# Writing out the turn loops of five graph layers and dropping a memset between gathers

## The reference, cut to what matters

```python
e = leaky_relu(alpha_s[src] + alpha_d[dst], 0.2)
m = segment_max(e, dst)
ex = exp(e - m[dst])
s = segment_sum(ex, dst)
alpha = ex / (s[dst] + 1e-16)
out = segment_sum(h[src] * alpha[:, :, None], dst)
```

## Time and profile before

| | us |
|---|---|
| timed, median of 3 runs | 7401.44 (7400.56 to 7405.69) |
| profiled execution, first to last instruction | 8931.6 |
| PE busy | 5412.5 (61%) |
| DVE busy | 4963.7 (56%) |
| ACT busy | 3871.5 (43%) |
| GpSimd busy | 5847.5 (65%) |
| mean granted TensorE clock | 0.745 |

### The profile page before, as it was taken

One profiled execution on the slowest core, in us unless ns is written; L12 is line 12 of the kernel. 1 busy time (PEld: TensorE's weight loads), 2 busy tenths in 40 slices (PEclk: granted clock), 3 DMA queues, 4 the chain that ended last, 5 costly groups with the idle time before them and its releaser, 6 DMA issues. The chain is left out here.

```text
span 8931.6 us, 130458 instructions
## 1 busy us (share of the span) xinstructions
PE 5412.5 (61%) x23088; PEld 4000.6 (45%) x23089; DVE 4963.7 (56%) x11653; ACT 3871.5 (43%) x9075; POOL 5847.5 (65%) x8186
## 2 busy tenths in 40 slices
PE   6442365666535656664676666658888754666665
PEld 5431244444424444443455555435555533444443
DVE  6444355555545555554677777744444445555556
ACT  2220255455424554552244444335555533454444
POOL 0555677777747777775467666657777765777774
PEclk9555677777767777776788988868888866777777
DMA  4112233333313333331466666423333323333332
GB/s 143 49 49 52 75 95 95 95 96 95 86 44 97 96 95 95 96 97 33 127 176 178 177 176 175 129 64 99 100 101 100 101 53 101 99 99 99 98 98 74
DMA packets 580940, 894.72 MB, mean 100 GB/s; under 512 B 307359, under 2 KB 357708, under 8 KB 580448
## 3 DMA queue, kind: packets, MB, share of 16 engines
q0 software_dynamic: 245984, 649.30, 26.7%
q1 hardware_dynamic: 334448, 218.84, 8.9%
q10 hardware_dynamic: 416, 25.60, 0.9%
HBM read 859.36 MB, written 59.47 MB: 103 GB/s over the span
## 5 line engine op out<-in xcount | busy, mean ns | idle before, releaser
L2002 POOL DMA_INDIRECT ad_ring<-tab_qv,ad_idx x808 | 770.7, 954 | 506.4 <-issue 217.6
L1515 POOL DMA_INDIRECT at_ring_0a<-tab_s,at_idx_0a x808 | 774.3, 958 | 430.9 <-PE at_po_0a L1680 219.2
L2396 POOL DMA_INDIRECT ae_ring<-tab_a,ae_idx x808 | 777.9, 963 | 423.0 <-PE ae_po L2553 233.7
L1515 POOL DMA_INDIRECT at_ring_0b<-tab_s,at_idx_0b x808 | 772.8, 956 | 426.7 <-PE at_po_0b L1680 213.2
L1515 POOL DMA_INDIRECT at_ring<-tab_s,at_idx x808 | 780.1, 965 | 377.6 <-PE at_po L1680 183.0
L1680 PE MATMUL at_po_0a<-at_rows_0a,at_hot_0a 128*128 128x264 f32 x1616 | 625.6, 560 | 520.8 <-ACT at_hr_0a L1780 199.8
L1680 PE MATMUL at_po_0b<-at_rows_0b,at_hot_0b 128*128 128x264 f32 x1616 | 624.3, 559 | 512.2 <-ACT at_hr_0b L1780 201.7
L1680 PE MATMUL at_po<-at_rows,at_hot 128*128 128x260 f32 x1616 | 614.5, 553 | 444.5 <-DVE acc L1566 179.0
L1680 PEld LDWEIGHTS at_po_0a<-at_rows_0a,at_hot_0a 128*128 128x128 f32 x1616 | 439.3, 282 | 670.8 <-DVE acc L1566 262.0
L1680 PEld LDWEIGHTS at_po_0b<-at_rows_0b,at_hot_0b 128*128 128x128 f32 x1616 | 438.5, 282 | 662.4 <-DVE acc L1566 264.4
L1680 PEld LDWEIGHTS at_po<-at_rows,at_hot 128*128 128x128 f32 x1616 | 435.9, 280 | 586.2 <-DVE acc L1566 225.4
(11 more groups left out here) (508 smaller groups left out, 14085.4 us busy)
## 6 DMA issues: line engine op xcount, KB each, us to landing
at_rr_0a<-relrow_d SPq DMA_DIRECT2D x102, 256.0 KB
at_rr_0b<-relrow_d SPq DMA_DIRECT2D x102, 256.0 KB
ad_rr<-relrow_d SPq DMA_DIRECT2D x102, 256.0 KB
at_rr<-relrow_s SPq DMA_DIRECT2D x102, 256.0 KB
ae_feat<-attr_pad SPq DMA_DIRECT2D x808, 32.0 KB
rnk_lrow<-lorow_f SPq DMA_DIRECT2D x98, 256.0 KB
attr_pad<-in_edge_attr_dram ACTq DMA_DIRECT2D x1, 25000.0 KB, 79.1
at_ring_0a<-tab_s,at_idx_0a POOLq DMA_INDIRECT x808
```

What stands on the lines that cost most here:

```text
L1515: eng.indirect_dma_start(out=ring[:, t.slot * STEP + u, :], out_offset=None, in_=table, in_offset=bass.IndirectOffsetOnAxis(ap=idx[:, t.sl ...
L2002: eng.indirect_dma_start(out=ring[:, t.slot * STEP + u, :], out_offset=None, in_=table, in_offset=bass.IndirectOffsetOnAxis(ap=idx[:, t.sl ...
L2396: eng.indirect_dma_start(out=ring[:, k, :], out_offset=None, in_=table, in_offset=bass.IndirectOffsetOnAxis(ap=idx[:, k:k + 1], axis=0))\
```

## The change

The `Fori` loops over turns become Python `range` loops in `attend` (SP, GpSimd, and `run`, which DVE, PE and ACT use), in `attend_dot` (the same) and in `aggregate_edges` (all five engines). Each turn is then in the program once for each time it runs, and every wait is for a constant. The tiles `pause`, the memsets that fill them and the semaphores `paused` with their waits and first increments are gone. The loops of the sort stay. Nothing that is computed changes.

```diff
-            pause = sb(f"at_pause_{tag}", [P, 2, QUAD, 2 * P], F32, c)
...
-                with eng.Fori(0, LAPS - 1) as i:
+                for i in range(LAPS - 1):
                     for k in range(1, BUFS + 1):
                         step(Turn(i, k), True, True, True)
...
                         for q in range(quads):
-                            eng.wait_ge(paused, t.n * STEP + (q * QUAD + QUAD))
                             eng.wait_ge(mat, m.at(f"mm{q * QUAD + QUAD - 1}", t.plus(-2)))
...
                                     .then_inc(landed[t.slot][q], 16)
-                                eng.memset(pause[:, q % 2, j, :], 0.0).then_inc(paused, 1)
-
-                    eng.sem_inc(paused, 2 * QUAD)
-                    with eng.Fori(0, LAPS - 1) as i:
+
+                    for i in range(LAPS - 1):
                         for k in range(BUFS):
                             gather(Turn(i, k), STEP // QUAD)
...
-                with step.eng.Fori(0, EVEN) as i:
+                for i in range(EVEN):
...
-            pause = sb(f"ae_pause_{tag}", [P, STEP, P], F32, c)
...
                     def gather(i, quads):
-                        eng.wait_ge(paused, i * STEP + STEP)
                         for q in range(quads):
                             eng.wait_ge(copied, i * (STEP // QUAD) + q + 1)
                             eng.wait_ge(summed, i * HALF + (q * 2 + 2))
...
-                                eng.memset(pause[:, k, :], 0.0).then_inc(paused, 1)
```

More of the change, by code:

```diff
@@ L1429, in attend @@
             v, s, m = Ops(vec, V, 3), Ops(act, A, 1), Ops(mat, M, 3)
-            paused, blank = ph.sem("at_paused"), ph.sem("at_blank")
+            blank = ph.sem("at_blank")
             moving = Scatter(f"at_{tag}", ph, c, scatter) if scatter else None
@@ L1976, in _ @@
                     step(turn(0, 0), True, True)
-                    with eng.Fori(0, EVEN) as i:
+                    for i in range(EVEN):
                         for k in range(1, BUF + 1):
@@ L2013, in _ @@
                     gather(turn(0, 1), False)
-                    with eng.Fori(0, TURNS // BUF - 1) as i:
+                    for i in range(TURNS // BUF - 1):
                         for k in range(BUF):
@@ L2379, in aggregate_edges @@
             far = ph.sem("ae_far")
-            paused = ph.sem("ae_paused")
             told, warmed = ph.sem("ae_told"), ph.sem("ae_warmed")
@@ L2398, in gather @@
                                     .then_inc(landed[k], 16)
-                                eng.memset(pause[:, k, :], 0.0).then_inc(paused, 1)
-                    eng.sem_inc(paused, STEP)
-                    with eng.Fori(0, TURNS - 1) as i:
+                    for i in range(TURNS - 1):
                         gather(i, STEP // QUAD)
```

## The result

The changed kernel takes 6980.27 us (6976.69 to 6984.77, 4 runs) against 7403.07 us (7400.56 to 7405.69): ratio 0.9431, 95% interval 0.9417 to 0.9444, a gain of 423 us. 7130 was forecast, a gain of 270. The way was right and the time lies in the range; the gain that was forecast was too small by a third.

What follows compares the result with a forecast made beforehand. GpSimd's gathers (23.0 us a turn) and the DVE, PE, ACT chain (22.4 to 23.3) were taken as close bounds. Gains of 120 (0a, 0b), 95 (last), 40 (edge) and 15 (query-key), 270 us, gave 7130; range 6930 to 7430.

Steps and rivals of the forecast that it cites:

- the chain: Turn's waits through DVE, PE and ACT: 22.4 us in the last stage's loop, 0.9 more in 0a and 0b.
- Both candidates fit in it: Timed attention turn of 21.9 to 23.3 us has room for GpSimd's 23.0 and the DVE, PE, ACT chain's 22.4.
- The memset: Attention gathers go from 1.44 to 1.25 us apart without it, GpSimd's floor from 23.0 to 20.0 us a turn.
- They go at no price: GpSimd's `paused` waits are met by its own earlier memsets, so nothing is late because of them.
- The edge term: Edge stage: GpSimd's floor falls by 1.1 us and register work goes; 0.8 us a turn taken, 40 us.
- I take 1.2: Register instructions ahead of waited-for additions cost 0 to 1.2 us a turn, from turns of 22.4 and 21.2; 1.2 taken.
- 0a and 0b heavier by 0.9: Chain in 0a and 0b 0.9 us longer than in the last stage: 23.3 looped, 22.1 straight, twice 60 us gained.
- GpSimd as the only bound: Rival: the memset's full worth comes in the attention and edge stages, 520 us, giving 6880; chance 0.09.
- Code loading: New straight code costs 0 to 0.5 us a turn, 0 taken; some 200 more packets for PE, about 250 for others.
- The query-key stage: `attend_dot`: GpSimd's 23.8 us a turn doesn't change, so unrolling gains 0 to 1.2; 0.3 taken, 15 us.
- the condition that I named as proof against that floor: If `attend_dot` gains as much as the other stages, GpSimd's floor there isn't one.
- Gathers without a pause: Rival: streaming gathers delay DVE's, PE's and ACT's waits, 384 us less 270, giving 7515; chance 0.10.

Runs made afterwards that it cites:

- flat_pause: The kernel before with all turn loops written out, memsets and the waits on them kept: 7336.81 us, ratio 0.9902 to before.
- loop_nopause: The kernel before with the loops kept, and the memsets, their tiles and the waits on them dropped: 7274.91 us, ratio 0.9816 to before.
- before_split: The kernel before, loops and memsets kept, with DVE's group numbers in attend loaded in four portions: 7334.29 us, ratio 0.9909 to before.
- flat_pe: loop_nopause with only PE's turn loops written out: 7140.78 us.
- flat_dve: loop_nopause with only DVE's turn loops written out: 7146.42 us.
- flat_act: loop_nopause with only ACT's turn loops written out: 7284.02 us.
- flat_movers: loop_nopause with only the loops of GpSimd and SP written out: 7280.83 us.
- loop_split: loop_nopause with DVE's group numbers in attend loaded in four portions: 7012.66 us, ratio 0.9470 to before.

## Why the prediction was right, and where it was off

**The bound.** That GpSimd's spacing and the chain stood close together was right: `flat_pause`, `loop_nopause` and `before_split` show each of them alone. "Both candidates fit in it" was argued from an execution that was a stray, which was luck in part; the floors of GpSimd survived because they were made of spacings within GpSimd's own stream, which were the same in both executions.

**The memset.** 1.44 to 1.25 us a gather, and a floor of 20.0, as forecast. Alone it was worth 0.1 us a turn in 0a and 0b (23.90 to 23.79, 23.93 to 23.84) and 0.4 in the last stage, since the looped chain of 23.8 and 22.9 took over; in attention its worth came with the loops.

**"They go at no price"** for the `paused` waits was a failed step. In attention it holds (turns of 23.1 to 23.2 with these waits against a floor of 23.0), in the edge stage it doesn't: 0.65 us a turn, because that wait is for the memset just issued. Of the edge turn's 2.11 us, 0.68 is that wait (22.12 to 21.44), 1.25 the memset (21.44 to 20.19), and 0.18 the loops (22.30 to 22.12). The edge term was sized 40 us and measured 105. I had taken 0.8 from between the bounds, where GpSimd's whole spacing was on the path: 1.25 a turn, not the 1.1 that I had from 1.27 us a gather; 0.96 + 0.30 is 1.26, as measured.

**The registers.** The term "I take 1.2", from two neighbouring turns of the last stage, measured 2.03 to 2.04 in 0a and 0b and 1.46 in the last stage (from `loop_nopause` to the changed kernel). The step that failed is the reading of one looped turn of 22.4 as the typical one. Looped turns came in two kinds, 22.2 and 24.0 us in the last stage of `loop_nopause`, by whether the clock fell ahead of the last quad. 22.4 was one of the short ones; the mean was 22.91. The straight turn of 21.2 was a short one too, where the mean of the changed kernel is 21.45. The place was wrong too: DVE's additions don't pay for the registers, three other places on DVE do, and on PE more than half of the gain goes with the clock.

**0a and 0b heavier by 0.9.** In loops they are (23.79 against 22.91 in `loop_nopause`); carrying the 0.9 over to straight turns was the error, where it is 0.3 (21.76 against 21.45). The forecast of 22.1 for the turn after was 0.3 too high, of 23.3 for the turn before 0.6 too low, which makes their 60 us each into 107. In the last stage 23.1 to 21.2 were both 0.2 too low, and the 95 us came out by that luck. The forecast's own range is off as well: half to one and a half times 270 gives 7266 to 6996, not 7280 to 6980, and the gain of 423 is beyond one and a half times 270. What held the time was the wider range, whose low end had been put there for a part of another case, GpSimd as the only bound.

**Code loading.** 155 more packets in PE's queue (27 to 182) and 262 more in the others' (65 to 327), where some 200 and 250 were forecast. That q8 is PE's queue shows in `flat_pe`, which raises q8 alone, from 27 to 182; `flat_dve`, `flat_act` and `flat_movers` raise q14 alone, from 63 to 192, 129 and 132. The packets cost nothing that shows: `flat_pe` has 155 more of them than `loop_nopause` and is 134 us faster, `flat_dve` 129 more and is 128 faster, and the straight turns of 0a and 0b are shorter than forecast (21.76 and 21.80 against 22.1; that of the last stage, 21.45, is longer than its 21.2). Taking 0 was right for this change: the loops of before brought 4 and 7 packets in all of stage 0a, so no loading was there to be saved, and the gain is found at DVE's waits and in PE's turns. A pass of PE's three turns has some 590 recorded instructions, weight loads among them, and runs with these 4 packets in the whole stage. Stops beside packets of code do appear on DVE in 0b and the last stage of `loop_split` and `before_split`, 3.2 to 5.4 us a pass. So "0" holds for this loop body, not for any.

**The query-key stage.** 23.83 to 23.81, 1 us in all against 15. GpSimd's floor holds it, and the condition that I named as proof against that floor didn't come about. The terms given for it, 16 x 1.25 and twice 2.00, add up to 24.0, not 23.8; a gather ahead of the weighing takes 0.97 instead of 1.25.

**The rivals.** Gathers without a pause delay nobody: DVE's wait at the additions, 5.35 us in the earlier trace rows, is 2.25 us in the changed kernel (at 1233.25), and the two turns under the 28 scatters take 21.7 and 20.3 us (`rescale` at 1908.37, 1930.05 and 1950.33), not the 48.1 of the earlier trace rows. That turn was the stray execution's.

## What to carry to other kernels

When two engines' times for a turn lie within a few per cent, price an edit for each and take the larger time that is left: either half of this change was worth 1 to 2% and both 5.7%, and the next edit on the chain gave 209 us after it but 65 before. When a profile's span is far from the timed median, take another profile before any waits are read from it; the spacings within GpSimd's own stream could still be used here, 1.44 us from gather to gather in 0a in the profile of 8931.6 us and in that of 7409.8. A wait of GpSimd for its own memset just issued cost 0.65 us, where the same wait on the memset of one turn before cost nothing (an edge turn of 21.44 against a floor of 21.4). And when one piece of looped code runs at two speeds in two stages, look for stops with no releaser and for packets on the instruction queues before the clock is blamed: in `loop_split` such stops were 60 of the 75 us between 0a and 0b.

## What was not expected of the hardware

The granted TensorE clock goes with 1.5 us of a turn: with PE's loop and the group numbers loaded in one go it fell ahead of the last quad, to a mean of 0.55 to 0.60 over the last four additions, in 20 to 29 of 50 attention turns, and in the changed kernel in 1 of 100 in 0a and 0b and in 9 of 50 in the last stage. In `loop_split` two stages of the same looped code ran at 20.97 us and 22.48 us a turn; in the slower one DVE stopped once a pass for 4.4 to 5.4 us, with 78 packets of code in 1040 us, and in the other there were 4 in 980 and no such stop. Writing out the loops of GpSimd, SP and ACT gained nothing that could be measured (7281 and 7284 against 7275 us).
